# A six-layer decoder on one core: 16-wide heads stacked through TensorE instead of through DRAM

## The chip, the cores and the metric

One core of one Trainium2 chip runs the whole program. The metric is the device time of one execution in microseconds, the median of the runs. TensorE (PE) multiplies and transposes into PSUM; ScalarE (ACT), VectorE (DVE) and GpSimd (POOL) do elementwise work, of which GpSimd can't reach PSUM; SyncE (SP) issues DMAs. Each engine runs its own instructions in order, and semaphores hold them together.

## What is computed

Four batches of 512 tokens with 256 features go through six residual layers: windowed attention, attention of latents to a context of 1024 tokens, a ternary feed-forward layer, self-attention with 16 heads of 16, cross-attention of the same heads to the context (256-wide, rotary embedding), and a routed feed-forward layer of eight experts. The change touches the fourth and the fifth:

```
x = x + _L1_attn_ref(_layernorm(x, axis=-1), ...)
x = x + _L1_xattn_ref(_layernorm(x, axis=-1), ctx_1024, ctx_1024, ...)

q = (x @ Wq.T + bq).reshape(b, s, NHEADS, DK)      # NHEADS = 16, DK = 16
k = (x @ Wk.T + bk).reshape(b, s, NHEADS, DK)
w = jax.nn.softmax(jnp.einsum('bshd,bzhd->bhsz', q, k) / jnp.sqrt(jnp.float32(DV)), axis=-1)
out = jnp.einsum('bhsz,bzhd->bshd', w, v).reshape(b, s, NHEADS * DV) @ Wo.T + bo
```

The fifth does the same with q, k after rotation by position (`apply_rope`) and with 1024 keys. All of it is single precision in the reference.

## The kernel before

Every float32 operand is kept as two 16-bit halves, an upper one and the rest (`dk[0]` and `dk[1]`), and a product is three matmuls: upper by upper, upper by lower, lower by upper (L563 to L571). Features lie on partitions, tokens along the free dimension.

A head has only 16 features, so one of its score products would use 16 of 128 rows of TensorE. The kernel stacks instead: `qs` and `ks` hold, for each of eight pairs of heads, 16 rows of upper q, 16 of lower q and 16 of upper q again, against upper, upper and lower k. One matmul over 48 rows (`HR`) then gives the whole three-part product of a head; the two heads of a pair stand at rows 0 and 64, so their matmuls run in different row groups at the same time. Rows 48 and 49 of each half carry the shift of the softmax in two parts (`shift_rows`, L471) against rows of 64s in `ks`.

Stacking moves data between partitions. Before, SyncE does it by DMA: `send` (L454) stores both halves of 128 features to a DRAM tensor (`kd`, `qd`), and `stack` (L461) reads each back in six DMAs, three parts for the even and three for the odd heads. A feature half c carries the pairs 4c to 4c+3. The rows of 64s come from DRAM too (`kc_d`, L449 to L452), once per batch.

Both attentions run in `attend`. First come the score slots: slot a is one pair of heads, one block of 128 queries and 512 keys, two matmuls into two PSUM banks (`score_slot`, L787), and VectorE takes the negated maximum of each (`max_slot`, L1524). Two slots are in flight. Self-attention has 8 slots in each of four groups, cross-attention 16. After one slot more than a group, its maxima are transposed (`shift_slot`), VectorE splits them (`shift_split`, L1536: L1543 and L1544) and SyncE puts them into rows 48 and 49. `mode.upto(0)` slots, 13 and 21, run ahead of the loop. In the loop TensorE computes the scores turned, keys on partitions (`turned_scores`, L829), ScalarE exponentiates (L1154), and TensorE weighs the values (`weigh`, L841, four heads in four column groups), while later slots run on in between.

The order of work ahead of the slots, self-attention: norm 6 (VectorE's moments; GpSimd's power -0.5, L551; VectorE's normalisation, four instructions at L1271), transposes of y, four projections (K and Q of the halves 0 and 1) into banks 2 to 5, four value products into banks 6 and 7; ScalarE takes the upper halves (L1173, L1175), VectorE the lower (L1619 to L1624). Then ScalarE and VectorE split the context that was loaded into `craw` (L1182, L1627). Cross-attention: six projections with their rotated partners (`rope_product`, two of them still inside the self-attention), `rotate` on VectorE with two rows of sums on VectorE (L1584) and four on GpSimd (L527), eight value products, four evictions of values.

SyncE's queue is in program order: the trips of K and Q, the four shifts of self-attention, the trips of the cross-attention, the load of the experts' weights (L503, over the memory of the context's halves and of `dk` and `dq`), its four shifts, the output. GpSimd splits the experts' weights when they have landed (`split_experts`).

`keep_warm` are eight or more matmuls whose result nobody reads, issued when the variance of a norm is ready. The letters W and C give a weight's halves and a bias column.

## Time and profile before

| | us |
|---|---|
| median of 3 runs | 2514.1 (2505.96 to 2517.42) |
| the profiled execution | 2511.27 |
| its span, first to last instruction | 2509.3 |
| TensorE busy (weight loads apart) | 2061.7 (82%) |
| VectorE busy | 1803.5 (72%) |
| ScalarE busy | 1251.6 (50%) |
| GpSimd busy | 186.8 (7%) |
| mean granted TensorE clock | 0.914 |

A busy time is the sum of an engine's instructions; a timeline row gives start, duration, engine, line and operation, and in brackets the idle time ahead of it with what ended it. The granted clock is 1.00 at 2.4 GHz and 0.50 at 1.2 GHz. The four batches take some 619 us each after the first; the stretch described here, from norm 6 to the last score slot ahead of the loop, lies in batch 1 between 983 and 1018 for self-attention and between 1075 and 1122 for cross-attention.

### The profile page before, as it was taken

To read this page: it belongs to the slowest core of one execution; us is meant where nothing else is said; L and a number is where in the kernel's file an instruction comes from. 1 tells how busy PE (TensorE), PEld (TensorE's weight loads), DVE (VectorE), ACT (ScalarE), POOL (GpSimd) and SP (SyncE) were. 2 spreads that over 40 slices of the span, in tenths; PEclk is the share of its full clock that TensorE was granted. 3 is DMA by queue.
4 is the path that set the end of the run, shared out by engine and by line. 5 is a ranking of instruction groups with operands and counts; after the bars stand their busy time and mean duration, and the time that the engine had idled before them with its cause. 6 is when DMAs were issued, how large, how long until landed. Compare 5 with 4: busy or idle time off the path is not lost.

```text
span 2509.3 us, 50443 instructions
## 1 busy us (share of the span) xinstructions
PE 2061.7 (82%) x17818; PEld 1155.0 (46%) x17818; DVE 1803.5 (72%) x2815; ACT 1251.6 (50%) x1862; POOL 186.8 (7%) x198
## 2 busy tenths in 40 slices
PE   3899867788889986869879997687987999758788
PEld 2567632324556663222446665332254667423225
DVE  7788677693678867687477885768657788676855
ACT  4466535275256644528325663452832666335382
POOL 1000000140000000022000000003100000000400
PEclk9999977889999998879999999787999999979799
DMA  6266601400136651040014664104001566310400
GB/s 233 48 124 119 113 19 44 130 2 10 35 66 118 125 111 31 14 130 2 9 35 84 124 120 94 43 2 130 2 9 35 104 118 124 75 42 10 122 2 9
DMA packets 441919, 173.91 MB, mean 69 GB/s; under 512 B 408553, under 2 KB 432241, under 8 KB 440817
## 3 DMA queue, kind: packets, MB, share of 16 engines
q1 hardware_dynamic: 441154, 169.33, 30.7%
q8 instruction: 114, 1.87, 0.3%
q0 software_dynamic: 576, 2.10, 0.3%
q14 instruction: 75, 0.61, 0.1%
HBM read 57.85 MB, written 12.60 MB: 28 GB/s over the span
## 4 chain that ended last, share of the span: by engine, by line
issue 69%; PE 9%; DVE 8%; POOL 6%; DMA 4%; SPq 3%; ACT 1%; POOLq 0%; DVEq 0%; ACTq 0%
POOL arena L540 3%; DVE nmx L1529 3%; DMA arena<-in_experts 2%; SPq L467 2%; PE ps L841 2%; POOL arena L538 2%; POOL rstd L551 1%; PE ps L829 1%; PE ps L568 1%; PE ps L570 1%; PE ps L569 1%; DVE y L1271 1%; PE ps L587 1%; SPq L459 1%; DVE quant L1435 0%
## 5 line engine op out<-in xcount | busy, mean ns | idle before, releaser
L1154 ACT ACTIVATE arena<-ps 128x512 f32<-128x512 f32 x768 | 402.9, 601 | 275.7 <-PE ps L829 266.8
L1529 DVE TENSOR_REDUCE nmx<-ps 128x2 f32<-128x1024 f32 x384 | 443.9, 1219 | 49.2 <-PE ps L797 47.7
L797 PE MATMUL ps<-arena 48*128 48x512 f16 x768 | 196.2, 488 | 102.5 <-DVE nmx L1529 64.3
L1359 DVE TENSOR_SCALAR_CACHE_REDUCE ps<-ps 128x1536 f32<-128x1536 f32 x128 | 225.9, 1765 | 39.6 <-PE ps L570 39.6
L841 PE MATMUL ps<-arena 128*17 128x256 f32 x3072 | 250.4, 402 | 0.0
L568 PE MATMUL ps<-arena 128*128 128x512 f16 (+2 forms) x672 | 226.6, 337 | 10.6 <-DVE arena L1334 4.8
L1372 DVE SCALAR_TENSOR_TENSOR arena<-arena,rs 128x1536 f16<-128x1536 f32 x128 | 231.6, 1809 | 4.4 <-ACT arena L1061 4.4
L569 PE MATMUL ps<-arena 128*128 128x512 f16 (+2 forms) x672 | 226.2, 337 | 0.0
L570 PE MATMUL ps<-arena 128*128 128x512 f16 (+2 forms) x672 | 225.7, 336 | 0.0
L1061 ACT ACTIVATE arena<-arena,rs 128x1536 f16<-128x1536 f32 x128 | 200.8, 1569 | 46.9 <-DVE rs L1365 46.9
L1053 ACT ACTIVATE arena<-ps,nm 128x1536 f32<-128x1536 f32 x128 | 197.0, 1539 | 29.5 <-DVE ps L1359 29.5
L829 PE MATMUL ps<-arena 50*128 50x512 f16 x768 | 193.8, 424 | 6.8 <-DMA arena<-arena 6.3
L684 PE MATMUL ps<-arena 128*128 128x128 f16 x1536 | 189.8, 222 | 2.1 <-DMA arena<-arena 2.1
L685 PE MATMUL ps<-arena 128*128 128x128 f16 x1536 | 189.9, 222 | 0.0
L577 PE MATMUL ps<-wh,ident 128*128 128x512 f16 x368 | 100.6, 430 | 89.7 <-DVE ve L1265 89.7
L551 POOL TENSOR_TENSOR rstd<-ve,col 128x4 f32<-128x4 f32 x36 | 37.9, 1053 | 1740.1 <-DVE ve L1265 1740.1
L684 PEld LDWEIGHTS ps<-arena 128*128 128x128 f16 x1536 | 152.3, 99 | 11.8 <-DMA arena<-arena 3.5
L685 PEld LDWEIGHTS ps<-arena 128*128 128x128 f16 x1536 | 152.6, 99 | 6.9
L568 PE MATMUL ps<-wh,arena 128*128 (+2 forms) x832 | 153.6, 224 | 0.2
L570 PE MATMUL ps<-wh,arena 128*128 (+2 forms) x832 | 152.0, 223 | 0.0
L569 PE MATMUL ps<-wl,arena 128*128 (+2 forms) x832 | 151.9, 223 | 0.0
L568 PE MATMUL ps<-arena,wh 128*128 128x512 f16 x320 | 123.3, 385 | 29.6 <-DVE arena L1347 14.8
(210 smaller groups left out, 3811.1 us busy)
## 6 DMA issues: line engine op xcount, KB each, us to landing
arena<-in_experts SPq DMA_DIRECT2D x4, 3840.0 KB, 13.6
arena<-in_weights SPq DMA_DIRECT2D x8, 929.0 KB, 14.4
arena<-qd SPq DMA_DIRECT2D x96, 64.0 KB, 2.4
arena<-kd SPq DMA_DIRECT2D x48, 128.0 KB, 4.3
arena<-in_ctx SPq DMA_DIRECT2D x4, 1024.0 KB, 6.1
arena<-arena SPq DMA_TRANSPOSE x256, 3.7
arena<-in_ctx_t SPq DMA_DIRECT2D x4, 1024.0 KB, 6.9
qd<-arena SPq DMA_DIRECT2D x32, 128.0 KB, 1.8
```

What stands on the lines that cost most here:

```text
L568: mm(out_, lh, rh, start=(k == 0), stop=False)
L569: mm(out_, lh, rl_, start=False, stop=False)
L570: last = mm(out_, ll, rh, start=False, stop=(k == n - 1))
L684: mm(d_, vh[:, kt, :], ph[:, kt, :], start=(kt == 0), stop=False)
L685: mm(d_, vl[:, kt, :], ph[:, kt, :], start=False, stop=False)
L829: mm(ps[:, 4 + n % 3, :], ks[rows, 2 * g_ + pp, P * kt:P * kt + P], qs[rows, 2 * g_ + pp, :], start=True, stop=True).then_inc(b_mm.sem, 1)
L841: mm(ps[32 * j:32 * j + VW, 7, cols], v17[:, kt, 4 * g_ + j, :], pr_[:, (4 * t + j) % RING, cols], start=(kt + half == 0), stop=(kt == mod ...
L1061: A(xq[i % 2][0], xp[:, i % 2, :], ACT.Copy, scale=rs[:, i:i + 1]).then_inc(s_hi.sem, 1)
L1154: A(pr_[:, n % RING, :], ps[:, 4 + n % 3, :], ACT.Exp).then_inc(b_exp.sem, 1)
L1359: TS_(s_, s_, -XS, None, ALU.mult, ALU.min, accum_out=nm[:, i:i + 1]).then_inc(s_max.sem, 1)
L1372: STT(xq[i % 2][1], xp[:, i % 2, :], rs[:, i:i + 1], xq[i % 2][0], ALU.mult, ALU.subtract).then_inc(s_lo.sem, 1)
L1529: V.tensor_reduce(nmx[:, g_ % 2, ch, :, pp, i], ps[:, 2 * (z % 2):2 * (z % 2) + 2, :], AX.X, ALU.max, negate=True)\
```

## The change

The DRAM tensors go, and with them `send`, `stack` and the row of 64s. A 16-bit matrix `sel` with ones, built once from `ident16`, has 128 columns for each of four kinds (K upper, K lower, Q upper, Q lower). A product of its 32 rows with the 32 features of a pair, once for the upper and once for the lower half, added up in one PSUM bank, is that pair's stacked operand. TensorE does it in `select_k` and `select_q`, one bank for 512 tokens, so K of the cross-attention takes two. ScalarE evicts K (`stacked_k`, which adds `k_pad`, the 64s in rows 48 and 49) and Q (`stacked_q`, in self-attention with the scale 1/4, which the projection no longer carries); pair 0 of Q is VectorE's (`first_q`).

The pairs 1 to 7 are made between the first slots, together with the values: in self-attention at slots 1 to 7 and 4, 6, 8, 10; in cross-attention pairs at odd slots and values at even ones. The fourth projection of self-attention is made behind slot 1. The last lower halves stand behind the first slots on VectorE too.

GpSimd splits the context (`split_context`), directly behind norm 6's power -0.5. On SyncE the first shift of the cross-attention moves ahead of the experts' load. Each group of slots now waits for its own pair instead of for a DMA.

```diff
+            nc.gpsimd.memset(sel[:], 0.0).then_inc(pads_set.sem, 1)
...
+            def split_context(b):
+
+                pool.wait_ge(craw_in.sem, craw_in.at(b, 16))
+                alone(pool)
+                for c in range(DC):
+                    nc.gpsimd.tensor_copy(crT[0][:, c, :], craw[:, c, :]).then_inc(cr_hi.sem, 1)
+                for c in range(DC):
+                    pool.wait_ge(cr_hi.sem, cr_hi.at(b, c + 1))
+                    alone(pool)
+                    nc.gpsimd.tensor_tensor(crT[1][:, c, :], craw[:, c, :], crT[0][:, c, :], ALU.subtract).then_inc(cr_lo.sem, 1)
...
                     nc.gpsimd.tensor_tensor(rstd[:], ve[:], col[:, COL["half"]:COL["half"] + NT], ALU.pow)\
                       .then_inc(rstd_ready.sem, 1)
+                    if k == 6:
+                        split_context(b)
...
-                if a == 2 * mode.per_group:
-                    pe.wait_ge(qk_in[1].sem, qk_in[1].at(b, 192 * (mode.m + 1)))
+                if i + ch == 0:
+                    n = LH // 2 * mode.m + 2 * g_ + pp + 1
+                    pe.wait_ge(k_st.sem, k_st.at(b, n))
+                    pe.wait_ge(q_st.sem, q_st.at(b, n))
...
+            def select(d_, src, kinds, p_, t0):
+
+                c, jj = divmod(p_, 4)
+                rows = slice(32 * jj, 32 * jj + 32)
+                for part in range(2):
+                    last = mm(d_, sel[rows, kinds + part, :], src[part][rows, c, t0:t0 + 512], start=(part == 0), stop=(part == 1))
+                return last
...
+            def between_self(b, a):
+
+                if a == 1:
+                    self_product(b, 3)
+                if 1 <= a < 8:
+                    select_k(b, 0, a)
+                    select_q(b, 0, a)
+                if a in (4, 6, 8, 10):
+                    self_value(b, (a - 4) // 2)
+
+            def between_cross(b, a):
+
+                if a % 2 and a < 14:
+                    select_k(b, 1, (a + 1) // 2)
+                    select_q(b, 1, (a + 1) // 2)
+                elif a and a % 2 == 0 and a <= 16:
+                    cross_value(b, a // 2 - 1)
...
+            def stacked_k(b, m_, p_):
+
+                act.wait_ge(sel_mm.sem, sel_mm.at(b, LH * m_ + 2 * p_ + 1))
+                n = (S, NCTX)[m_]
+                A(ks[:, p_, 0:n], banks(4, 1 + m_), ACT.Identity, bias=k_pad[:]).then_inc(k_st.sem, 1)
...
-                for c in range(DC):
-                    send((lq_lo, 2 * c + 1), kd, dk, S, c, k_out)
-                    send((lq_lo, 2 * c + 2), qd, dq, S, c, q_out)
-                    stack(k_out, 2 * c + 2, kd, ks, S, c)
-                    stack(q_out, 2 * c + 2, qd, qs, S, c)
...
+                shift_rows(MODES[1], 0)
+                for done, n in ((lv_mm, 6), (k_st, LH), (q_st, LH)):
+                    sp.wait_ge(done.sem, done.at(b, n))
+                    alone(sp)
                 sp.dma_start(arena[:, HE:HE * 2 * NE], moe_in[:, 0:HE * (2 * NE - 1)]).then_inc(raw_in.sem, 16)
                 sp.dma_start(raw_last, moe_in[:, HE * (2 * NE - 1):HE * 2 * NE]).then_inc(raw_in.sem, 16)
-                for g_ in range(GROUPS):
+                for g_ in range(1, GROUPS):
                     shift_rows(MODES[1], g_)
```

On TensorE the program before has, at the end of self-attention's products, the last value product (three matmuls of it shown), and then the score slots alone (L797), each behind a wait:

```order
L568 MATMUL ps<-wh,yT_hi 128x256
L569 MATMUL ps<-wl,yT_hi 128x256
L570 MATMUL ps<-wh,yT_lo 128x256
L856 ISA
L857 ISA
L797 MATMUL ps<-arena 128x512 x4
L794 ISA
L797 MATMUL ps<-arena 128x512 x2
L794 REGISTER_ALU
L797 MATMUL ps<-arena 128x512 x2
```

In the changed program the same place, from slots 3 and 4 on (L772; selections are L860, products L540 to L542):

```order
L772 MATMUL ps<-arena 128x512 x2
L869 REGISTER_ALU
L860 MATMUL ps<-arena,sel 128x512 x4
L769 REGISTER_ALU
L772 MATMUL ps<-arena 128x512 x2
L869 REGISTER_ALU
L860 MATMUL ps<-arena,sel 128x512 x4
L540 MATMUL ps<-wh,yT_hi 128x256
L541 MATMUL ps<-wl,yT_hi 128x256
L542 MATMUL ps<-wh,yT_lo 128x256
```

Four selections, and behind every second slot a value product, stand between two slots that stood side by side before.

On GpSimd the program before goes from norm 6's power straight to the sum of the rotation, norm 7's power and the other sums:

```order
L551 TENSOR_TENSOR rstd<-ve,col 128x4
L526 ISA
L527 TENSOR_TENSOR arena<-arena 128x512
L549 REGISTER_ALU
L551 TENSOR_TENSOR rstd<-ve,col 128x4
```

and the changed one has the context's four operations in between:

```order
L521 TENSOR_TENSOR rstd<-ve,col 128x4
L491 ISA
L494 CAST arena<-arena 128x1024 x2
L496 ISA
L498 TENSOR_TENSOR arena<-arena 128x1024
L496 REGISTER_ALU
L498 TENSOR_TENSOR arena<-arena 128x1024
L485 ISA
L486 TENSOR_TENSOR arena<-arena 128x512
```

They need only `craw`, loaded since the second layer, and so start right behind the power.

## Rows read from the trace of the kernel before

**Rows 1.** The page: busy time, share of the span, instructions of each engine

```profile
PE 2061.7 (82%) x17818; PEld 1155.0 (46%) x17818; DVE 1803.5 (72%) x2815; ACT 1251.6 (50%) x1862; POOL 186.8 (7%) x198
```

**Rows 2.** Waits: engine, line, whom for; total us, times, longest

```profile
PE ps L797 <- DMA arena<-qd: 38.2, 8, 5.9
```

**Rows 3.** Timeline of TensorE, self-attention of batch 1: start, duration, [idle before]

```profile
988.59 0.39 PE L568 MATMUL ps<-yT_hi,wh 128*128 128x512 f16 x1 [1.58 <-DVE yT_lo L1292]
...
996.29 0.27 PE L570 MATMUL ps<-wh,yT_lo 128*128 128x256 f16 x1
1002.18 1.04 PE L797 MATMUL ps<-arena 48*128 48x512 f16 x4 [5.62 <-DMA arena<-qd]
...
1017.61 0.61 PE L829 MATMUL ps<-arena 50*128 50x512 f16 x2 [0.73 <-DMA arena<-arena]
```

**Rows 4.** Timeline of SyncE's queue, same stretch

```profile
997.63 2.70 SPq L467 DMA_DIRECT2D arena<-qd  x6
```

**Rows 5.** Timeline of VectorE, same stretch

```profile
984.48 1.38 DVE L1271 TENSOR_SCALAR y<-x,mv,rstd 128x256 f32<-128x256 f32 x4 [1.12 <-POOL rstd L551]
...
990.81 0.75 DVE L1619 SCALAR_TENSOR_TENSOR arena<-ps,col,arena 128x512 f16<-128x512 f32 x1 [2.05 <-ACT arena L1173]
...
1002.85 10.28 DVE L1529 TENSOR_REDUCE nmx<-ps 128x2 f32<-128x1024 f32 x9 [2.32 <-PE ps L797]
1013.04 0.27 DVE L1543 TENSOR_SCALAR arena<-ps 16x128 f16<-16x128 f32 x1
```

**Rows 6.** Timeline of ScalarE: a projection's upper half; eight exponentials in a run

```profile
990.09 0.69 ACT L1173 ACTIVATE arena<-ps,col 128x512 f16<-128x512 f32 x1 [2.40 <-PE ps L570]
...
1144.92 4.41 ACT L1154 ACTIVATE arena<-ps 128x512 f32<-128x512 f32 x8 [0.25 <-PE ps L829]
```

**Rows 7.** Timelines of TensorE and VectorE, cross-attention of batches 1 and 3

```profile
1097.95 0.60 PE L797 MATMUL ps<-arena 48*128 48x512 f16 x4 [4.74 <-DMA arena<-qd]
...
1090.30 0.69 DVE L1584 TENSOR_TENSOR arena<-arena 128x512 f32<-128x512 f32 x1
...
1098.41 18.20 DVE L1529 TENSOR_REDUCE nmx<-ps 128x2 f32<-128x1024 f32 x16 [6.03 <-PE ps L797]
...
1117.88 0.27 DVE L1543 TENSOR_SCALAR arena<-ps 16x128 f16<-16x128 f32 x1
...
2329.20 0.69 DVE L1584 TENSOR_TENSOR arena<-arena 128x512 f32<-128x512 f32 x1
...
2335.84 18.20 DVE L1529 TENSOR_REDUCE nmx<-ps 128x2 f32<-128x1024 f32 x16 [4.56 <-PE ps L797]
```

**Rows 8.** GpSimd beside VectorE: timelines; last, durations in ns (min/median/max) of L1534

```profile
1076.61 1.64 POOL L527 TENSOR_TENSOR arena<-arena 128x512 f32<-128x512 f32 x1 [0.32 <-DVE arena L1579]
...
1077.05 2.32 DVE L1271 TENSOR_SCALAR y<-x,mv,rstd 128x256 f32<-128x256 f32 x4
...
L1534 DVE TENSOR_TENSOR nmx<-nmx x16: 174/176/886, 502.0 to 2414.8; 128x16 f32<-128x16 f32 x16
```

**Rows 9.** Timeline of GpSimd, the experts' halves of 512 columns

```profile
1116.83 0.61 POOL L538 CAST arena<-arena 128x512 f16<-128x512 f32 x1 [31.30 <-DMA arena<-in_experts]
1117.52 1.15 POOL L540 TENSOR_TENSOR arena<-arena 128x512 f16<-128x512 f32 x1
```

**Rows 10.** Timeline of TensorE at full clock: scores, weighing (four column groups), turned scores

```profile
1027.20 0.38 PE L797 MATMUL ps<-arena 48*128 48x512 f16 x2
1027.51 0.62 PE L841 MATMUL ps<-arena 128*17 128x256 f32 x8
1028.07 0.45 PE L829 MATMUL ps<-arena 50*128 50x512 f16 x2
```

**Rows 11.** Windows: stretch, us; busy PE, PEld, DVE, ACT, POOL; PEclk, DMA share, GB/s

```profile
1000.00:1005.00 5.00, 1.64 (x6) 0.23 (x6) 2.68 (x3) 0.00 (x0) 0.00 (x0) 0.50 0.58 181
...
1020.00:1025.00 5.00, 4.42 (x22) 0.91 (x20) 4.73 (x6) 3.37 (x7) 0.00 (x0) 0.50 0.00 0
```

**Rows 12.** Timeline of VectorE, the first norm behind the weights' last half

```profile
37.15 1.39 DVE L1253 BATCH_NORM_STATS2 st<-y 128x6 f32<-128x256 f32 x4
```

More of the change, by code:

```diff
@@ L238, in decoder @@
         o32 = lay.take([2, S])
+        raw_last = lay.take([HE])
         assert lay.at <= 57344
@@ L245, in decoder @@
         sh = lay.take([2, 2, P], F16)
-        raw_last = lay.take([HE])
         lay = Layout()
@@ L852, in output_slot, with self_product, self_value @@
                 last.then_inc(sl_mm.sem, 2)
+            def self_product(b, j):
+                name, m = ("sk", "sq")[j % 2], j // 2
+                product(ps[:, 4 + j, :], [(W(name, c, P * m, P), both(yT, slice(None), c)) for c in range(DC)])\
+                    .then_inc(lq_mm.sem, 1)
+            def self_value(b, i):
+                if i == 0:
+                    pe.wait_ge(lq_lo.sem, lq_lo.at(b, 2 * DC))
+                last = product(ps[:, 6 + i // 2, D * (i % 2):D * (i % 2) + D],
+                               [(both(yT, slice(None), c, slice(P * i, P * i + P)), W("sv", c, 0, D)) for c in range(DC)])
+                if i % 2:
+                    last.then_inc(lv_mm.sem, 1)
@@ new lines, in cross_value @@
+            def cross_value(b, i):
+                if i % 2 == 0 and i:
+                    pe.wait_ge(lv_hi.sem, lv_hi.at(b, 2 + i // 2))
+                last = product(ps[:, 7, D * (i % 2):D * (i % 2) + D],
+                               [(both(crT, slice(None), c, slice(P * i, P * i + P)), W("cv", c, 0, D)) for c in range(DC)])
+                if i % 2:
+                    last.then_inc(lv_mm.sem, 1)
+            def select(d_, src, kinds, p_, t0):
[4 more added lines that the diff above has]
+                return last
@@ new lines, in select_k @@
+            def select_k(b, m_, p_):
+                if p_ % 4 == 0:
+                    split, n = ((lq_lo, 2 * (p_ // 4) + 1), (rp_lo, 2 * (p_ // 4) + 2))[m_]
+                    pe.wait_ge(split.sem, split.at(b, n))
+                if p_:
+                    pe.wait_ge(k_st.sem, k_st.at(b, LH // 2 * m_ + p_))
+                elif m_:
+                    pe.wait_ge(rp_mul.sem, rp_mul.at(b, 5))
+                for ch in range(1 + m_):
+                    last = select(ps[:, 4 + ch, :], dk, 0, p_, 512 * ch)
+                last.then_inc(sel_mm.sem, 1)
@@ L892, in self_attention @@
                 pe.wait_ge(y_lo.sem, y_lo.at(b, 12))
-                for j, (name, m) in enumerate([("sk", 0), ("sq", 0), ("sk", 1), ("sq", 1)]):
-                    product(ps[:, 2 + j, :], [(W(name, c, P * m, P), both(yT, slice(None), c)) for c in range(DC)])\
-                        .then_inc(lq_mm.sem, 1)
-                for i in range(NT):
-                    last = product(ps[:, 6 + i // 2, D * (i % 2):D * (i % 2) + D],
-                                   [(both(yT, slice(None), c, slice(P * i, P * i + P)), W("sv", c, 0, D)) for c in range(DC)])
-                    if i % 2:
-                        last.then_inc(lv_mm.sem, 1)
+                self_product(b, 0)
+                self_product(b, 1)
+                select_k(b, 0, 0)
+                self_product(b, 2)
+                select_q(b, 0, 0)
                 attend(b, 0)
@@ L920, in cross_attention @@
                 pe.wait_ge(lx_added.sem, lx_added.at(b, NT))
-                for i in range(NCTX // P):
-                    last = product(ps[:, TILE_BANK[i // 2], D * (i % 2):D * (i % 2) + D],
-                                   [(both(crT, slice(None), c, slice(P * i, P * i + P)), W("cv", c, 0, D)) for c in range(DC)])
-                    if i % 2:
-                        last.then_inc(lv_mm.sem, 1)
+                select_k(b, 1, 0)
+                select_q(b, 1, 0)
                 attend(b, 1)
@@ L1248, in _ @@
                 weights_lo(k)
+            dve.wait_ge(pads_set.sem, 10)
+            own.link(V.tensor_reduce(sel_row[:], ident16[:].rearrange("p (j s) -> p s j", j=4), AX.X, ALU.max))
+            src = sel_row[:].rearrange("p (e d) -> p e d", e=2)
+            for kind, r_ in ((0, 0), (0, 1), (1, 2), (2, 0), (2, 2), (3, 1)):
+                dst = sel[:, kind, :].rearrange("p (e n) -> p e n", e=2)[:, :, LD * r_:LD * r_ + LD]
+                TS_(dst, src, 1.0, None, ALU.mult).then_inc(sel_set.sem, 1)
+            pad = ident[:].rearrange("p (e n) -> p e n", e=2)[:, :, HR:SR]
+            own.link(V.tensor_reduce(k_pad[:], pad, AX.XY, ALU.add))
+            own.link(TS_(k_pad[:], k_pad[:], 64.0, None, ALU.mult))
             dve.wait_ge(b2_hi.sem, 1)
@@ L1593, in attend @@
                 mode = MODES[m_]
-                slots(b, mode, 0, mode.upto(0))
+                for a in range(mode.upto(0)):
+                    slots(b, mode, a, a + 1)
+                    if m_ == 0 and a < 2:
+                        self_lo(b, 2 + a)
+                    elif m_ == 1 and a == 0:
+                        rotated_lo(b, 5)
                 for t in range(mode.steps):
```

159 lines of the change are left out of this document (77 added, 82 removed).

## The prediction

> **What bounds the kernel now.** I read the shares of the page first, then the waits, then one batch's self-attention and its cross-attention engine by engine. TensorE is busy 82% of the span, VectorE 72%: neither is the bound everywhere, the bound changes by stage [rows 1]. The waits name what the change removes: TensorE stood idle 38.2 us in 8 places, two per batch, for a DMA out of qd [rows 2]. The reader should see in batch 1 (the second): the last product ends at 996.5, the first score matmul starts at 1002.18 [rows 3]; SyncE meanwhile issues DMAs one after another, 2.7 us for six [rows 4]. From then VectorE's maxima bound the stretch, 10.28 us for nine, up to the shift at 1013.04 [rows 5]; the turned scores wait for the shift's DMA, until 1017.61 [rows 3]. Cross-attention is alike: 4.74 us idle up to 1097.95, first maximum 1098.41, shift 1117.88 [rows 7]. So what counts is when the shift is computed: everything behind it (loop, output, norm) starts from there and is unchanged. VectorE's start of the shift is my yardstick.
>
> **Self-attention, up to the first maximum.** The six DMAs and the two sends of each half go; the last wait is then a chain of products and evictions. From the first product (988.59) 24 matmuls of 512 columns and 24 of 256, as much as 36 of 512, end at 996.5: 0.22 each, and I work with 0.216 [rows 3]. Two products of six end at 2.6. ScalarE's upper halves (0.69) and VectorE's lower halves (0.75), with some 0.2 to 0.24 from TensorE to the other engine [rows 3, 5, 6], end at 4.3. The first K selection (two matmuls, 0.43) stands before the third product, which ends at 4.7; the Q selection at 5.15; VectorE evicts it (0.75) by 6.1; score slot, 0.22 plus 0.24: first maximum at 6.6. Before it was 14.26. **Gain 7.6.**
>
> **From there to the shift.** Before, 10.2 us. Now TensorE carries in the same stretch the fourth product (1.3), seven pairs of selections (4 x 0.216) and two value products (0.65 each), and switches between a matmul over 32, over 64 and over 128 rows. A switch costs: at full clock a score pair's 512 columns are 0.22, but from its start to that of the four-column form it is 0.31, and that form (0.43 of columns) lasts 0.56 [rows 10]: 0.11 a switch. One step is then 0.22 + 0.86 + 0.22 = 1.30, and ScalarE's two evictions (0.55 each at a run's pace, with a hand-over after each) about the same; both are above VectorE's 1.13. Two score slots and the product 1.85, seven steps 9.1, two value products 1.5, and about 1.3 for hand-overs and the ninth maximum, make 13.8: **3.6 lost**. Net gain 4.0 if nothing else happens.
>
> **The context's halves on GpSimd.** On ScalarE and VectorE they were free, in the shadow of the DMAs. GpSimd does them right after the reciprocal root of norm 6, that is while VectorE normalises y in four instructions (1.38 us), and y must be whole before TensorE can transpose. What such a neighbour costs is in [rows 8]: GpSimd's sum ran from 1076.61 to 1078.25, and VectorE's normalisation, begun at 1077.05, took 2.32 instead of the 1.38 of [rows 5]: it got in only when GpSimd was done. A tiny minimum of VectorE has a median of 0.176 and a longest of 0.886; the long ones lie under GpSimd's subtractions of the experts. So an instruction waits for the whole of the other's, and at a boundary the one that waited gets in. New are two casts and two subtractions of 1024 columns; of 512 they take 0.61 and 1.15 [rows 9], so 1.04 to 1.22 and 2.0 to 2.3. The first normalisation starts with the root's end; the first cast falls between it and the second, the second cast between second and third, the first subtraction before the fourth: 1.04 + 1.04 + 2.0 = **4.1 us later**. Bounds: 0.9 (one wait as in [rows 8]) and 4.7. I take 4.1 since in the row GpSimd, which had waited for the VectorE operation before, got in ahead of the normalisation that was already due. The Trainium skill (SBUF — State Buffer, Who interferes with whom) says that the port pair the two share is an exclusive lock for the whole instruction, and that tensor_scalar in its two-port mode takes it; the trace agrees. It also says that issue order decides who blocks; were VectorE to keep the port over its four instructions, this term and the clock's would be 0 and the sum 28 us lower.
>
> **The clock.** In that longer gap TensorE has only its eight filler matmuls, then 4.7 us nothing. After an idle stretch of that kind its clock was at 1.2 GHz: granted 0.50 from 1000 to 1005, after 5.6 us idle [rows 3, 11]. So the transposes and the first products run partly at half speed. Working the chain above through with 0.427 per matmul for the time that a low stretch then lasts gives 2.8 us (bounds 0 and 5). The later low stretch (granted 0.50 until the weighing sets in) I expect again, since TensorE idles between slots nine to thirteen and the shift's DMA as before: no term. Self-attention is then 4.0 - 4.1 - 2.8 = **-2.9, a loss**.
>
> **Cross-attention.** First maximum: the rotated sum of the last Q half starts some 0.15 earlier than before (1090.30 [rows 7]), the first Q selection waits for the lower half of the other, then eviction 0.75 and slot: maximum at about 1092.05 instead of 1098.41, 6.35 gained; in batch 3 the distance from that sum to the first maximum is 6.64 instead of 8.11 [rows 7], so 4.9 there; mean 5.6. The last lower half (0.65) now stands between the first two maxima. Per pair of slots TensorE has two slots 0.43, six selections 1.30, a value product 0.65 and four switches 0.44: 2.82 against VectorE's 2.27; seven pairs lose 3.9, less 0.9 that the second bank buffers: 3.0. 5.6 - 0.65 - 3.0 = **+2.0** (bounds: 5 with free switches, -3 if each of the 42 selections costs 0.1 more).
>
> **The rest.** The experts' load goes behind the first shift on SyncE's queue and starts at once after it, so the shift's last rows may land later: no row shows it; between 0 and 1.5 us, I take 0.4. It lands 12 us later than before, GpSimd's 32 us of expert halves then end near 1160, 60 us before they are needed; they meet one more of VectorE's small minima, 0.7 in half the batches at most: 0.2. Prologue: VectorE builds sel (a reduction, six small copies, a reduction and a product, each 0.1 to 0.25) in front of the first norm, which follows the weights without a gap [rows 12]: +1.2 once. GpSimd's 6.9 us of filling the row of 64s and its store were hidden.
>
> **Sum.** Per batch -2.9 + 2.0 - 0.6 = 1.5 us lost; 4 x 1.5 + 1.2 = 7. The profiled execution took 2511.3 (span 2509.3), 2.8 below the median of 2514.1: 2511.3 + 7 = **2518 us**. That is inside 0.5% (12.6 us), about what a measurement of this kernel can tell from no change.
>
> **Rivals.**
> *The port costs little (faster).* The first cast comes too late for the first boundary, or VectorE keeps the port: self-attention keeps 2 to 4 us, and with switches hidden by the row groups' overlap cross-attention 4.5. 4 x (3 + 4.5 - 0.6) = 28, less 1.2: 2485. For it: the two matmuls of a score pair do run side by side, a start to the next form within 0.31 [rows 10]. Against: [rows 8].
> *The clock does not carry the selections (slower).* They use 32 of 128 rows. Matmuls over 48 and 50 rows left the clock at 0.50 from 1020 to 1025 though TensorE was 88% busy [rows 11]. If selections count as little, the clock falls in the slots and stays: a self step is 1.71 + 0.43 + 0.28 = 2.4 instead of 1.3, 7 x 1.1 = 8; a cross pair twice 2.38 plus 0.5 of switches, 5.3 instead of 2.82, 17. 4 x 25 = 100 more: 2618. It decides from the first step in which selections alone fill TensorE. The Trainium skill (TensorE: Matmul & The Clock Gate, What's actually happening) speaks of how busy the engine has been, not of rows; by that the rival falls.
> *Selections do not pipeline (slower).* If loading sel is not hidden behind a matmul over the same rows, 0.1 on each of some 70 selections a batch, 5 of 7 us on the path: 2538. The products' 0.216 with a new weight each speaks against.
> *The trips go, but nothing is gained* because the selections fill the freed time: that is the forecast's own neighbour, 2511 to 2518.
>
> **Chances.** Forecast and its neighbours (2502 to 2526) 0.45; port cheap 0.25; pipelining or more low clock (2527 to 2550) 0.20; clock lost altogether 0.10. Leaving out that last and the best of the second gives 2486 to 2550. Faster by over 0.5% 0.25, within 0.45, slower 0.30.
>
> **What would show it.** In the profile after: four normalisations of norm 6 at about 5.5 us instead of 1.38 (port); first maximum 6.6 us after the first product when the clock is full; pairs of slots 2.3 or 2.8 us apart in cross-attention; granted clock in the slots 1.00 or 0.50; turned scores 4.3 us behind the shift. The forecast is wrong if the normalisation is not delayed, or if selections run at half clock.

## The result: slower by 3.8%

The changed kernel takes 2605.2 us (median of 4, 2600.4 to 2614.5) where the kernel before takes 2510.2: ratio 1.038, 95% interval 1.034 to 1.042. The forecast was 2518 with a range up to 2550; the rival "the clock does not carry the selections" had given 2618. The profiled execution took 2600.4 (span 2597.9) at a mean granted clock of 0.891 instead of 0.914.

The page of the changed kernel, busy times (answers [rows 1]):

```profile
PE 2228.0 (86%) x18138; PEld 1196.0 (46%) x18138; DVE 1820.6 (70%) x2816; ACT 1333.7 (51%) x1974; POOL 204.8 (8%) x214
```

and groups by line (busy time, mean ns of one | idle time before): two of the changed kernel, and last the maxima of the kernel before:

```profile
L860 PE MATMUL ps<-arena,sel 32*128 32x512 f16 x320 | 130.2, 554 | 5.4 <-DVE arena L1672 5.1
L1608 DVE TENSOR_REDUCE nmx<-ps 128x2 f32<-128x1024 f32 x384 | 450.6, 1221 | 130.4 <-PE ps L772 129.3
...
L1529 DVE TENSOR_REDUCE nmx<-ps 128x2 f32<-128x1024 f32 x384 | 443.9, 1219 | 49.2 <-PE ps L797 47.7
```

TensorE is busy for 166 us more. A recorded selection takes 554 ns on average; at full clock it is some 380 (below). Records of neighbours overlap, so both are longer than the time from one to the next. The wait for qd is gone [rows 2], but VectorE's maxima now wait 129 us for TensorE's scores, where they waited 48 before (in self-attention 2.3 us at the head of a run of nine [rows 5]).

VectorE in batch 1 (answers [rows 5] and [rows 7]): the normalisation of norm 6, first maximum and shift of self-attention; then maxima of cross-attention and its shift:

```profile
1006.90 6.39 DVE L1350 TENSOR_SCALAR y<-x,mv,rstd 128x256 f32<-128x256 f32 x4 [1.12 <-POOL rstd L521]
...
1024.90 1.23 DVE L1608 TENSOR_REDUCE nmx<-ps 128x2 f32<-128x1024 f32 x1 [0.59 <-PE ps L772]
...
1044.26 0.27 DVE L1622 TENSOR_SCALAR arena<-ps 16x128 f16<-16x128 f32 x1
...
1135.50 1.23 DVE L1608 TENSOR_REDUCE nmx<-ps 128x2 f32<-128x1024 f32 x1 [0.71 <-PE ps L772]
...
1140.65 1.23 DVE L1608 TENSOR_REDUCE nmx<-ps 128x2 f32<-128x1024 f32 x1 [0.71 <-PE ps L772]
...
1163.73 0.27 DVE L1622 TENSOR_SCALAR arena<-ps 16x128 f16<-16x128 f32 x1
```

Two losses are in it. The normalisation takes 6.39 instead of 1.38 us, and a pair of cross-attention's slots takes 1140.65 - 1135.50 = 5.15 us where 2.82 was forecast. The windows say why (stretch, then busy time of PE first, and the granted clock before the last two columns; answers [rows 11]):

```profile
1028.00:1030.00 2.00, 2.00 (x10) 0.42 (x8) 2.00 (x3) 1.59 (x4) 0.00 (x0) 1.00 0.00 0
1030.00:1032.00 2.00, 2.00 (x7) 0.52 (x6) 1.93 (x2) 1.19 (x3) 0.00 (x0) 0.57 0.00 0
1032.00:1046.00 14.00, 14.00 (x47) 4.25 (x46) 5.91 (x8) 5.57 (x9) 0.00 (x0) 0.50 0.00 0
...
1130.00:1150.00 20.00, 20.00 (x64) 6.53 (x62) 9.59 (x8) 7.59 (x10) 0.00 (x0) 0.50 0.00 0
```

TensorE has work in every moment, and its clock is at 1.2 GHz. In self-attention it even falls from 1.00 to 0.50 while the engine is busy without a gap (2.00 of 2.00 us in both windows). TensorE's own rows there, the selections of two steps (four matmuls each) and a score pair between them:

```profile
1029.22 1.09 PE L860 MATMUL ps<-arena,sel 32*128 32x512 f16 x4
1030.24 0.60 PE L772 MATMUL ps<-arena 48*128 48x512 f16 x2
1030.77 1.88 PE L860 MATMUL ps<-arena,sel 32*128 32x512 f16 x4
```

My theory after this: selections over 32 rows do not hold the clock, TensorE at 1.2 GHz then sets the pace of the slots, and GpSimd's split costs 5 us per batch besides. The rivals: it is the amount of work and its gaps, not the rows; or one of the two losses causes the other.

### The profile page after: what moved, and what is told of

Read it like the earlier page. It is cut to its first block, busy times and chain, and to the rows that moved or that the text cites. A ratio compares the mean times of both kernels' runs of the same rounds, so it can differ in the third digit from the quotient of the medians.

```text
span 2597.9 us, 51080 instructions
## 1 busy us (share of the span) xinstructions
PE 2228.0 (86%) x18138; PEld 1196.0 (46%) x18138; DVE 1820.6 (70%) x2816; ACT 1333.7 (51%) x1974; POOL 204.8 (8%) x214
## 4 chain that ended last, share of the span: by engine, by line
issue 67%; PE 18%; POOL 6%; DVE 6%; DMA 2%; ACT 1%; SPq 1%; POOLq 0%; DVEq 0%; ACTq 0%
PE ps L860 5%; POOL arena L510 3%; DVE nmx L1608 2%; PE ps L540 2%; PE ps L772 2%; PE ps L541 2%; PE ps L542 2%; PE ps L818 2%; DMA arena<-in_experts 2%; POOL arena L508 1%; DVE y L1350 1%; POOL rstd L521 1%; PE ps L806 1%; PE ps L559 1%; DMA ident<-in_eye 0%
## 5 line engine op out<-in xcount | busy, mean ns | idle before, releaser
L1608 DVE TENSOR_REDUCE nmx<-ps 128x2 f32<-128x1024 f32 x384 | 450.6, 1221 | 130.4 <-PE ps L772 129.3
L540 PE MATMUL ps<-arena 128*128 128x512 f16 (+2 forms) x672 | 226.1, 336 | 10.5 <-DVE arena L1413 4.7
L542 PE MATMUL ps<-arena 128*128 128x512 f16 (+2 forms) x672 | 225.3, 335 | 0.0
L772 PE MATMUL ps<-arena 48*128 48x512 f16 x768 | 182.7, 472 | 14.7 <-DVE arena L1710 7.0
L806 PE MATMUL ps<-arena 50*128 50x512 f16 x768 | 188.3, 417 | 6.6 <-DMA arena<-arena 5.7
L549 PE MATMUL ps<-wh,ident 128*128 128x512 f16 x368 | 108.5, 457 | 90.4 <-DVE ve L1344 90.4
L540 PE MATMUL ps<-wh,arena 128*128 (+2 forms) x832 | 162.3, 234 | 0.2
L542 PE MATMUL ps<-wh,arena 128*128 (+2 forms) x832 | 161.5, 235 | 0.0
L541 PE MATMUL ps<-wl,arena 128*128 (+2 forms) x832 | 161.4, 235 | 0.0
L540 PE MATMUL ps<-arena,wh 128*128 128x512 f16 x320 | 123.5, 386 | 26.2 <-DVE arena L1426 14.8
```

Of the source, the lines that this page charges most:

```text
L540: mm(out_, lh, rh, start=(k == 0), stop=False)
L541: mm(out_, lh, rl_, start=False, stop=False)
L542: last = mm(out_, ll, rh, start=False, stop=(k == n - 1))
L772: mm(ps[:, 2 * (z % 2) + e, :], qs[rows, 2 * g_ + pp, P * i:P * i + P], ks[rows, 2 * g_ + pp, 512 * ch:512 * ch + 512], start=True, stop=T ...
L806: mm(ps[:, 4 + n % 3, :], ks[rows, 2 * g_ + pp, P * kt:P * kt + P], qs[rows, 2 * g_ + pp, :], start=True, stop=True).then_inc(b_mm.sem, 1)
L1608: V.tensor_reduce(nmx[:, g_ % 2, ch, :, pp, i], ps[:, 2 * (z % 2):2 * (z % 2) + 2, :], AX.X, ALU.max, negate=True)\
```

## The experiments

One table first. It gives, for batch 1 of each run, the time from norm 6's normalisation to the first shift of self-attention, and from norm 7's to the first shift of cross-attention, both from VectorE's timeline (for the changed kernel 1044.26 - 1006.90, and 1163.73 - 1108.72, the latter the start of norm 7's). They are the two stretches that the change touches. The ratio is to the kernel before on the same chip. In the other batches they differ from this by 2.3 us or less, apart from the third batches of e2 and e7, which are told below.

| kernel | us | ratio (95%) | self | cross |
|---|---|---|---|---|
| before | 2510.2 | 1 | 28.6 | 40.8 |
| changed | 2605.2 | 1.038 (1.034 to 1.042) | 37.4 | 55.0 |
| e1: 128 rows | 2512.7 | 1.001 (1.000 to 1.002) | 32.3 | 39.6 |
| e2: context later | 2563.2 | 1.023 (1.019 to 1.026) | 29.1 | 55.2 |
| e3: both | 2488.4 | 0.992 (0.989 to 0.995) | 25.3 | 40.7 |
| e4: before, GpSimd's split alone | 2535.9 | 1.011 (1.009 to 1.013) | 36.5 | 41.7 |
| e5: 64 rows | 2570.8 | 1.024 (1.021 to 1.026) | 31.7 | 54.4 |
| e7: 32 rows, fillers in the slots | 2637.2 | 1.050 (1.047 to 1.052) | 36.4 | 62.6 |
| e8: 64 rows, fillers ahead of the slots | 2503.0 | 0.999 (0.997 to 1.000) | 31.7 | 38.4 |
| e12: 32 rows, fillers ahead of the slots | 2539.3 | 1.011 (1.009 to 1.013) | 37.4 | 39.5 |
| e6: e3, values late | 2465.2 | 0.983 (0.981 to 0.986) | 24.1 | 36.3 |
| e9: e6, fillers in the loop | 2458.2 | 0.980 (0.978 to 0.983) | 24.2 | 38.5 |
| e10: e9, fillers in the gaps | 2453.0 | 0.977 (0.976 to 0.979) | 23.3 | 36.3 |
| e11: before, fillers | 2498.2 | 0.995 (0.993 to 0.997) | 28.4 | 40.3 |

### e1: the same selections over 128 rows

```diff
-                rows = slice(32 * jj, 32 * jj + 32)
+                rows = slice(0, P)
                 for part in range(2):
-                    last = mm(d_, sel[rows, kinds + part, :], src[part][rows, c, t0:t0 + 512], ...)
+                    at = (LD, LD + 4 * P, 0, 3 * LD + 4 * P)[kinds + part] + P * jj
+                    last = mm(d_, sel[rows, at:at + P], src[part][rows, c, t0:t0 + 512], ...)
```

> The changed kernel with each selection over all 128 rows of dk or dq instead of its own 32; the other 96 rows of the selection matrix are zeros. As many matmuls, as many columns, the same operands out of them; the rows of a head stand in another order (lower, upper, upper for Q). Theory (rows): selections over 32 rows do not hold TensorE's clock, so it falls to 1.2 GHz while the engine is busy without a gap, and TensorE then bounds the slots. With 128 rows the granted clock in the cross-attention's slots is 1.00 instead of 0.50, a selection 0.22 us instead of 0.43 (or 0.63 for the recorded one), pairs of slots 2.3 to 2.9 us apart instead of 5.15, the step of self-attention 1.3. Per batch some 8 us in self-attention and 16 in cross-attention come back: 2605 - 96 = 2509, between 2495 and 2525. GpSimd's delay of norm 6 stays (four normalisations in 6.4 us). Rival (the amount of work, not its rows): the selections, their weight loads and the switches between forms are simply too many, and the clock falls for the gaps between them; then nothing changes, 2605 within 10, and pairs stay 5.15 apart at 0.50.

Measured 2512.7, 92 us less. VectorE's maxima in cross-attention, and a window over them:

```profile
1107.74 2.36 DVE L1608 TENSOR_REDUCE nmx<-ps 128x2 f32<-128x1024 f32 x2 [0.45 <-PE ps L771]
1110.55 2.36 DVE L1608 TENSOR_REDUCE nmx<-ps 128x2 f32<-128x1024 f32 x2 [0.45 <-PE ps L771]
...
1100.00:1116.00 16.00, 16.00 (x90) 6.65 (x90) 13.92 (x12) 10.16 (x14) 0.00 (x0) 1.00 0.01 2
```

A pair takes 2.81 us, with TensorE busy in all 16 us of the window at 1.00, and a recorded selection takes 382 ns on average. There are as many matmuls and as many columns, and three quarters of the rows have weights of zero: the rival "amount of work" is out.

### e2 and e3: GpSimd's split behind the normalisation

```diff
                     if k == 6:
+                        pool.wait_ge(y_ready.sem, y_ready.at(b, 6))
                         split_context(b)
```

e2 is the changed kernel with this edit, e3 has this and e1's.

> The changed kernel with one wait more: GpSimd splits the context only when VectorE has normalised norm 6 (y_ready). Theory (port): the four normalisations take 1.4 us again instead of 6.4, the chain behind them starts 5.0 us earlier, and as TensorE idles less there its clock may be up sooner: 5 to 8 us per batch, 2605 - 20 to 32 = 2573 to 2585. GpSimd's casts then run beside the transposes' evictions and the first maxima, which read PSUM and do not meet them; no reduction is longer than before. Rival (given back later): since TensorE is at 1.2 GHz in the slots whatever precedes them, or since VectorE's fp32 subtractions in the slots now meet GpSimd instead, half of it or more comes back as a delay: 2595 or more.

> Both edits: selections over 128 rows, and the context split behind norm 6's normalisation. Theory (rows and port, which add up): 2605 - 96 - 20 to 32 = 2477 to 2489, below the kernel before by 1%. If the low clock had only one of the two as its cause (the gap ahead of the transposes starts it, the selections prolong it), this is no faster than the better of the two single edits by more than 10 us. If the rows do nothing, it is as the edit of the wait alone, 2573 to 2585.

e2 measured 2563.2, 42 less than the changed kernel, more than the 20 to 32 expected. Norm 6's normalisation is whole again:

```profile
1001.07 1.38 DVE L1351 TENSOR_SCALAR y<-x,mv,rstd 128x256 f32<-128x256 f32 x4 [1.12 <-POOL rstd L521]
```

Of the 10.4 us of batch 1, 8.3 are in the self column: 5.0 the normalisation, 2.0 the clock up to the first maximum (18.0 us from normalisation to maximum fall to 11.0), 1.3 the slots. Nothing was given back. In the third batch the self column fell by more, from 37.4 to 24.9. There the clock did not fall in self-attention's slots at all, with the same code; the window over them:

```profile
1644.00:1658.00 14.00, 13.57 (x71) 4.45 (x69) 11.91 (x14) 9.41 (x16) 0.00 (x0) 1.00 0.00 0
```

e3 measured 2488.4: 24 us below e1, and below the kernel before. Windows over the entry to its slots in cross-attention:

```profile
1084.00:1086.00 2.00, 2.00 (x9) 0.65 (x6) 1.93 (x3) 0.30 (x1) 0.00 (x0) 0.65 0.00 0
1086.00:1088.00 2.00, 2.00 (x9) 0.85 (x8) 1.90 (x2) 1.30 (x2) 0.00 (x0) 0.50 0.00 0
1088.00:1090.00 2.00, 2.00 (x13) 0.65 (x10) 1.57 (x2) 0.37 (x1) 0.00 (x0) 1.00 0.00 0
```

Here the clock did fall, behind TensorE's two waits, and slots with 128-row selections raised it again. So it went in all four batches of e3. The waits do not decide it alone: in e1, with the same code there, TensorE waited 1.49 and 0.88 us, and the clock stayed up in all four batches. Windows of e1 over them:

```profile
1094.00:1096.00 2.00, 0.60 (x2) 0.11 (x2) 1.90 (x4) 1.08 (x2) 0.00 (x0) 1.00 0.00 0
1096.00:1098.00 2.00, 1.51 (x9) 0.65 (x10) 1.41 (x2) 0.21 (x1) 0.00 (x0) 1.00 0.00 0
```

### e4: one part of the change alone

In the kernel before, ScalarE's and VectorE's splits of the context are removed and `split_context` stands behind norm 6's power on GpSimd, as in the change.

> The kernel before with one part of the change alone: GpSimd splits the context directly behind norm 6's power, and ScalarE and VectorE no longer do. Theory (port): norm 6's normalisation takes 6.4 us instead of 1.4, everything behind it is 5.0 us later, and nothing is given back since the old splits lay in the shadow of the DMA trips: 2510 + 20 = 2530, with 1 to 3 us more per batch if TensorE's clock falls in the longer gap, up to 2541. Rival (absorbed): the projections or the trips take up part of the delay, or VectorE gets the port first when nothing else differs: 2510 to 2517.

Measured 2535.9, 27 us or 6.9 per batch. GpSimd's rows, and beside them VectorE's normalisation, first two of its instructions and then all four:

```profile
989.14 2.08 POOL L535 CAST arena<-arena 128x1024 f16<-128x1024 f32 x2
991.19 4.28 POOL L539 TENSOR_TENSOR arena<-arena 128x1024 f16<-128x1024 f32 x2
...
989.22 2.15 DVE L1280 TENSOR_SCALAR y<-x,mv,rstd 128x256 f32<-128x256 f32 x2 [1.12 <-POOL rstd L562]
...
989.22 6.39 DVE L1280 TENSOR_SCALAR y<-x,mv,rstd 128x256 f32<-128x256 f32 x4 [1.12 <-POOL rstd L562]
```

VectorE's first two instructions end 0.15 us after the two casts, its last two 0.14 us after the two subtractions: each of the four waited for one GpSimd operation. That is 5.0 us, and the self column grows by 7.9; the other 2.9 (1.6 to 2.3 in the other batches) fall where TensorE's clock is low behind the longer gap.

### e5 and e8: 64 rows, without and with fillers ahead of the slots

e5 against e1:

```diff
-                rows = slice(0, P)
+                rows = slice(64 * (jj // 2), 64 * (jj // 2) + 64)
```

> As the run with 128 rows, but each selection over 64 rows (its own 32 and the 32 zeros beside them), and GpSimd's split of the context as in the changed kernel. Theory (rows): what holds the clock is how much of the array the matmuls use; 64 rows are between the 32 that lost it (2605) and the 128 that held it (2512.7). With values in between (128 rows) I expect the cross-attention's slots at 1.00 for at least a part, pairs 2.8 apart there, and 2515 to 2560. Rival (any selection over fewer than 128 rows counts as nothing, or what hurt was the form of a 32-row matmul): 2605 in the first case with pairs 5.15 apart, 2512 in the second with every pair 2.8 apart.

Measured 2570.8, above the 2515 to 2560 expected, and the two attentions came apart, in all four batches. The windows over the slots of self-attention and of cross-attention:

```profile
1012.00:1032.00 20.00, 18.04 (x94) 6.28 (x93) 14.92 (x17) 11.98 (x20) 0.00 (x0) 1.00 0.00 0
1112.00:1146.00 34.00, 34.00 (x114) 12.00 (x112) 18.24 (x16) 12.99 (x17) 0.00 (x0) 0.50 0.00 1
```

The same form holds the clock in one and is at half speed for 34 us in the other. A difference is the entry: cross-attention's slots come behind two waits of TensorE for VectorE (1.39 and 0.87 us). So e8 fills these:

```diff
                 select_k(b, 1, 0)
+                keep_warm(5, 2)
                 select_q(b, 1, 0)
+                keep_warm(3, 2)
                 attend(b, 1)
```

> The run with selections over 64 rows, with eight matmuls over 128 rows that nobody reads in the two places where TensorE waits for VectorE ahead of cross-attention's first slot (idle 1.39 and 0.87 us there). In the run without them self-attention's slots, at 64 rows, stayed at 1.00, and cross-attention's, entered through that gap, were at 0.50 to the end. Theory (64 rows hold a clock that is up, but do not raise one that is down): without the gap the clock does not fall, cross pairs are 2.8 apart instead of some 5, and 12 to 15 us per batch come back: 2571 - 50 to 60 = 2511 to 2521. Rival (64 rows do not hold it in cross-attention, gap or no gap, since scores, values and selections mix in another way there): the clock falls some us later, in the slots, and the run is at 2560 to 2575.

Measured 2503.0: eight matmuls per batch that nobody reads brought 68 us, more than the 50 to 60 expected. TensorE's rows, and the window over the slots:

```profile
1089.07 1.25 PE L548 MATMUL ps<-wh,ident 128*128 128x512 f16 x5
1090.44 0.60 PE L860 MATMUL ps<-arena,sel 64*128 64x512 f16 x2
1090.97 0.82 PE L548 MATMUL ps<-wh,ident 128*128 128x512 f16 x3
...
1092.00:1112.00 20.00, 19.15 (x118) 8.65 (x117) 18.61 (x17) 12.68 (x17) 0.00 (x0) 1.00 0.00 1
```

Selections over 64 rows leave a clock that is up where it is, and do not raise one that is down.

### e7: fillers between the slots, 32 rows

```diff
+                if p_:
+                    keep_warm(1, 4)
                 for ch in range(1 + m_):
                     last = select(ps[:, 4 + ch, :], dk, 0, p_, 512 * ch)
```

and the same ahead of each Q selection.

> The changed kernel, selections over 32 rows as they are, with one more matmul of 512 columns over 128 rows ahead of each K and each Q selection of the pairs 1 to 7, into the bank that the selection then overwrites; nobody reads it. This only adds work: 112 matmuls. Theory (rows): the added matmuls bring the clock back, and more work takes less time: cross pairs 2.82 + 2 x (0.22 + 0.11) = 3.5 apart instead of 5.15, self steps 1.9 instead of 2.4 to 3; 12 to 13 us per batch, 2605 - 50 = 2555, between 2535 and 2580. If two in nine matmuls over 128 rows are too few, or under the rival (the amount of work and the gaps), each adds 0.43 at the low clock: 28 x 0.43 = 12 us per batch, 2605 + 48 = 2653.

Measured 2637.2, 32 more than the changed kernel: the expectation of the theory missed, and the rival's 2653 is nearer. Its windows over the slots of batch 1, and one over self-attention's slots of the third batch:

```profile
1036.00:1052.00 16.00, 16.00 (x71) 4.54 (x68) 9.84 (x10) 9.85 (x16) 0.00 (x0) 1.00 0.00 0
1132.00:1176.00 44.00, 44.00 (x127) 11.80 (x124) 18.54 (x16) 13.78 (x17) 0.00 (x0) 0.50 0.00 1
...
1690.00:1710.00 20.00, 20.00 (x53) 4.28 (x53) 5.62 (x6) 7.02 (x11) 0.00 (x0) 0.50 0.00 0
```

In self-attention it did what was expected in three batches of four: the clock stays at 1.00 where the changed kernel lost it, and the self column is 36.4 instead of 37.4 in batch 1 in spite of the added work. In the third batch the clock fell all the same, and the column is 45.4. In cross-attention the clock was already at 0.50 at the first slot, and two fillers to six selections did not raise it, so each cost its time there. I had put the fillers at the wrong place, as e8 shows.

### e12: the same gap filled, 32 rows

The changed kernel with e8's two added lines.

> The changed kernel, selections over 32 rows, with the same eight matmuls ahead of cross-attention's first slot that brought the 64-row run from 2571 to 2503. Theory (32 rows neither raise the clock nor hold it): in self-attention's slots the clock fell from 1.00 without an idle stretch ahead; so it will fall in cross-attention's slots too, some us after the fillers, and pairs are 5.15 apart from there: 2595 to 2605. Rival (the gap is what loses the clock, whatever the rows): the clock stays up, 15 us per batch come back, 2540 to 2555.

Measured 2539.3, close to the rival's 2540 to 2555; my theory of the rows falls for cross-attention. Windows over self-attention's slots and cross-attention's:

```profile
1010.00:1012.00 2.00, 1.92 (x11) 0.40 (x9) 2.00 (x3) 1.79 (x4) 0.00 (x0) 1.00 0.00 0
...
1014.00:1028.00 14.00, 14.00 (x44) 4.31 (x43) 6.59 (x7) 5.88 (x10) 0.00 (x0) 0.50 0.00 0
...
1110.00:1128.00 18.00, 17.63 (x103) 7.54 (x104) 15.78 (x15) 11.89 (x17) 0.00 (x0) 1.00 0.01 1
```

With the gap filled, 32-row selections keep the clock at 1.00 in cross-attention in all four batches (39.5 to 39.7 us in the cross column), where a value product of six matmuls over 128 rows stands in each pair of slots. In self-attention, whose first selections follow one another without a value product, they lose it from 1.00 with next to no gap ahead (1.92 of 2.00 us busy). Whether the value products make that difference was not tried.

So there are two causes, not one. In cross-attention the clock is lost at the entry, and slots with selections over 32 or 64 rows never raised it, in all 16 passes of the changed kernel, e2, e5 and e7; with 128 rows it either did not fall (e1) or came back (e3). In self-attention it is lost in the slots, and there the rows matter: with 32 rows it fell in 11 of the 12 passes of the changed kernel, e2 and e12, with 64 or 128 rows in none of the 16 of e1, e3, e5 and e8. The one exception, e2's third batch, shows that 32 rows do not always lose it; what else decides stays open.

### e6, e9, e10: what more the full clock is worth

e6 is e3 with the value products behind the selections, where VectorE's maxima cover them:

```diff
-                elif a and a % 2 == 0 and a <= 16:
-                    cross_value(b, a // 2 - 1)
+                if a >= 13:
+                    cross_value(b, a - 13)
```

with self-attention's at slots 8 to 11, and the wait for their evictions moved to the first weighing.

> The run with both edits (2488.4), with the value products moved behind the selections: cross-attention's eight at slots 13 to 20 instead of 2 to 16, self-attention's four at slots 8 to 11 instead of 4 to 10, and the wait for their evictions at the first weighing for cross-attention. Theory (with the clock up, TensorE's work between slots sets the pace): cross pairs go from 2.81 to VectorE's 2.27 to 2.4, 24.0 us from the first maximum to the shift to 20.5 to 21; self-attention 13.7 to 12.2. 4 x 5 = 20 us, less 0 to 8 for turned scores that now wait for the values: 2468 to 2476. Rival (given back behind the shift): the values and their evictions stand between the shift and the turned scores, so these start as late as before: 2484 to 2492. A third outcome: with less work between the slots the clock falls there again: slower than 2500.

Measured 2465.2, 23 us less than e3. VectorE's maxima of cross-attention run without waiting, thirteen in a row:

```profile
1076.17 15.00 DVE L1609 TENSOR_REDUCE nmx<-ps 128x2 f32<-128x1024 f32 x13
```

From first maximum to shift it is 21.0 us in cross-attention and 12.5 in self-attention, near the 20.5 to 21 and 12.2 expected. Over the four batches these two stretches gave some 16 of the 23 us; most of the rest came ahead of cross-attention's first maximum, where the clock fell in all batches of e3 and in only one of e6. e9 adds `keep_warm(2, 7)`, behind a wait for the values' evictions, to each of the second to fourth half steps of the loop, and e10 the fillers of e8 and eight more behind norm 7's transposes.

> The fastest so far (2465.2: both edits, values late) with six matmuls over 128 rows that nobody reads in the first two steps of each attention's loop, where TensorE has only matmuls over 48 and 50 rows (the weighing starts with the third step). Its profile shows the clock falling there, to 0.50 from 1005 to 1011.5 and from 1103.5 to 1110.5, with TensorE busy all the time and each half step 1.96 us instead of 1.1. Theory (rows): six matmuls over 128 rows keep it at 1.00; they cost 0.22 each where ScalarE's exponentials set the pace, and 2 to 3 us per attention come back: 2465 - 16 to 24 = 2441 to 2449. Rival (six are too few, or the fall comes from idle time): the clock falls all the same, each costs 0.43, 2 us more per attention: 2475 to 2485.

> The fastest so far (2458.2) with 16 more matmuls over 128 rows that nobody reads, per batch, in the waits ahead of cross-attention: eight while VectorE takes the lower half of norm 7's y (idle 2.10 us), five and three in the two waits ahead of the first slot. Its profile shows the clock at 0.50 from 1064.5 to 1068.2 and from 1074.5 to 1078.3 behind those waits. Theory: the clock does not fall there; the projections behind norm 7 and the first slots run at full speed, 1.7 and some 1.5 us: 2458 - 4 x 3 = 2446, between 2440 and 2452. Rival (only moved: the next fall comes at the next gap): 2455 to 2462.

e9 measured 2458.2, 7 us less than e6 where 16 to 24 were expected. The loop's start does run at full clock now (e6 from 1005 to 1011, e9 from 1002 to 1012):

```profile
1005.00:1011.00 6.00, 5.66 (x38) 0.96 (x38) 4.28 (x6) 3.25 (x6) 0.00 (x0) 0.50 0.01 1
...
1002.00:1012.00 10.00, 8.94 (x72) 2.54 (x72) 9.90 (x11) 8.29 (x16) 0.00 (x0) 1.00 0.01 2
```

and from the first to the last shift of self-attention it is 29.8 instead of 32.2 us. But batch 1 fell to 0.50 at two later gaps, and the cross column grew by 2.2. e10 filled those: back to 36.3, and 2453.0 us, 5 less where 12 were expected. This is 2.3% faster than the kernel before and 5.8% than the changed one.

### e11: how much of it is the clock alone

The kernel before with 16 fillers ahead of the wait for the stacked operands, two behind each slot ahead of the loop, six while the shift travels and six in the loop's first steps.

> The kernel before, nothing of the change, with matmuls over 128 rows that nobody reads where TensorE waits: 16 ahead of the wait for the stacked operands, two behind each slot ahead of the loop, six while the shift travels, six in the loop's first steps. It asks how much of the fastest runs' gain (2458 against 2507) is the clock alone. In the profile of before the clock is at 0.50 from the first slot to 1027, where half steps at the loop's start take about 2 us instead of 1.1. Theory: the slots gain nothing (VectorE sets their pace at either clock), the loop's start gains 2 to 3 us per attention: 2507 - 16 to 24 = 2483 to 2491, so that about half of the gain is the clock and half the trips through DRAM. Rival (the fillers delay scores or turned scores by as much as they bring): 2500 to 2510.

Measured 2498.2 (0.995, 0.993 to 0.997), 13 us instead of the 16 to 24 expected: self-attention's four shifts lie 30.3 us apart in all instead of 32.4, cross-attention's gain only 0.7. So of e10's 58 us on the same chip this placing of fillers has 13 without the change. The rest came with stacking through TensorE, with its clock up.

## Why the prediction was wrong, point by point

The first point rests on two windows of the kernel before, over the maxima of self-attention and of cross-attention. VectorE works almost all the time, TensorE about half of it:

```profile
1003.00:1013.00 10.00, 5.05 (x18) 0.87 (x16) 10.00 (x9) 0.00 (x0) 0.00 (x0) 0.50 0.31 88
1098.00:1117.00 19.00, 9.68 (x34) 1.62 (x34) 18.56 (x18) 0.00 (x0) 0.17 (x1) 0.51 0.96 284
```

- **The step that failed** is the time of a selection in the section "From there to the shift" and in cross-attention's pairs: 0.216 us, the full clock's, for slots in which the trace of before showed 0.50 [rows 11]. I expected "the later low stretch again" and wrote "no term" for it. That had been true only because VectorE set the slots' pace before: TensorE was busy about half of the time there, and half speed cost nothing. The change made TensorE the bound of the same stretch, and so the clock got a price: four selections that take 1.09 us in the changed kernel's row at 1029.22 take 1.88 in the one at 1030.77, and with the clock kept up (e1) 92 us came back. The rival named this mechanism and its size (cross pair 5.3, measured 5.15; 2618, measured 2605), with a chance of 0.10. [rows 11] held the evidence for more: 88% busy over 48 and 50 rows, and 0.50.
- That rival's account was half right. It said that the clock falls in the slots since selections use 32 of 128 rows. That is so in self-attention, though not in every pass (e1, e2, e7). In cross-attention it is lost at the entry, and filling TensorE's waits there keeps it (e8, e12). By the Trainium skill (TensorE: Matmul & The Clock Gate, What's actually happening), which goes by how busy the engine is, the rival fell; here the measurement decides otherwise: busy in 20.00 of 20.00 us, granted 0.50.
- **The sum at full clock was right.** With the clock up, first product to first maximum is 988.14 - 981.45 = 6.7 us in e3 (6.6 forecast), first maximum to shift 13.7 in e1 and e3 (13.8), a cross pair 2.81 (2.82). e1 is nearest to the kernel that I had priced: 2512.7 against the forecast's 2518. That its total fits is in part luck. Over its four batches self-attention lost 3.2 us (2.9 forecast) and cross-attention gained 1.2 (2.0), and 1.0 us per batch came back between the first and the last shift of self-attention, a stretch that I had called unchanged.
- **The port**: 5.0 us instead of 4.1, above the upper bound of 4.7. The mechanism of [rows 8] was right, but I had let VectorE in before the last subtraction. It got in after it (e4). The Trainium skill (SBUF — State Buffer, Who interferes with whom) has it that the first to issue holds the shared pair for its whole instruction. The trace agrees: in e4 the first GpSimd cast began at 989.14, ahead of VectorE's 989.22. My rival, in which VectorE keeps the port through its four instructions with a gain of 28 us, did not come true: the two engines took turns.
- **The clock behind that gap**: 2.0 us between e1 and e3 in batch 1 (18.6 against 11.6 to the first maximum, less 5.0) and up to 2.9 in the others, 1.6 to 2.9 in e4; 2.8 forecast. In batch 1 port and clock cost 5.0 + 2.0 = 7.0 where 4.1 + 2.8 = 6.9 were forecast; that the sum fits is luck, two errors cancel.
- **Smaller terms.** The first norm begins at 38.53 instead of 37.15, 1.4 us later (1.2 forecast). The turned scores of cross-attention start 4.6 us behind the shift in the changed kernel and 4.5 before: the experts' load ahead cost 0.1, not 0.4. Cross-attention kept 1.2 us in e1 (40.8 to 39.6), not 2.0: the first maximum came 4.6 us earlier instead of 5.6, and the slots cost 3.4 where the terms gave 3.65.
- **The range.** It left out the lost clock as the least likely case. Stretches whose bound the change moves from VectorE to TensorE should have been priced at the clock that they had, and the full clock kept as the hopeful case.

## What to carry to other kernels

Before giving TensorE work in a stretch where another engine sets the pace, read the granted clock of that stretch: a low clock is free only as long as TensorE is not the bound. Narrow matmuls left a low clock low here even when they filled the engine, so look at what stands ahead of them, fill that gap with full-height matmuls, or write a narrow matmul over all 128 rows with zeros, which cost no time here. And look at what VectorE does in the very microseconds into which work is moved to GpSimd: here one wait on the right semaphore was worth 42 us in e2 and 24 in e3.

## What the runs showed of the hardware

- The granted clock depends on the form of the matmuls and not on busy time alone: with the same number of columns, selections over 128 rows ran at 1.00 (16.00 of 16.00 us busy), over 32 rows at 0.50 (20.00 of 20.00 us). Rows whose weights are zero count. It does not depend on the form alone either: behind e12's fillers 32-row selections ran at 1.00 in cross-attention (17.63 of 18.00 us busy). Whether rows or something that goes with them (power, data) is what the chip looks at was not tried.
- To hold and to raise are two things: selections over 64 rows stayed at 1.00 for 20 us, and in the next attention at 0.50 for 34 us, with the same code.
- A matmul over 128 rows takes no longer than over 32: the shortest recorded selection takes 376 ns in e1 and 374 in the changed kernel; the mean of 554 there is the clock.
- VectorE's four normalisations waited through four GpSimd operations in turn, one for each, 6.39 us for 1.38 us of work. VectorE's maxima, which read PSUM, kept their time throughout: 1212 to 1228 ns for all 384 in the changed kernel, some 100 of them beside GpSimd's casts and subtractions.
